# An attention and FFN block on one core: the row maxima transposed by VectorE instead of TensorE

## The reference

```python
qkv = jnp.einsum('bsd,ed->bse', x, W_qkv)
q, k = _rope(q, positions), _rope(k, positions)
scores = jnp.einsum('bhqd,bhkd->bhqk', q, k) / jnp.sqrt(jnp.float32(dk))
scores = jnp.where(causal, scores, -jnp.inf)
out = jnp.einsum('bhqk,bhkd->bhqd', jax.nn.softmax(scores, axis=-1), v)
x = _layernorm(x + out @ W_o.T)
x = _layernorm(x + x @ simulate_quantize_int4(kernel) + bias + (x @ a) @ b)
```

## Time and profile before

| | us |
|---|---|
| median of 3 runs | 448.7 (448.59 to 451.78) |
| the profiled execution | 448.93 |
| its span | 446.9 |
| busy: TensorE, VectorE, ScalarE, POOL | 419.6, 378.9, 317.4, 119.4 |

### The profile page before, as it was taken

How to read it: one execution, slowest core, us unless ns; L and a number is a source line. 1 busy time by engine, 2 the same in 40 slices (tenths; PEclk the granted TensorE clock), 3 DMA queues, 4 the chain that set the end, 5 groups by cost and what they waited for, 6 DMA issues and landing times.

```text
span 446.9 us, 8486 instructions
## 1 busy us (share of the span) xinstructions
PE 419.6 (94%) x3198; PEld 204.5 (46%) x3198; DVE 378.9 (85%) x491; ACT 317.4 (71%) x643; POOL 119.4 (27%) x188
## 2 busy tenths in 40 slices
PE   5989899799799999999999999999999999999873
PEld 2546445334334445454443544544353445535352
DVE  2888799899989999998999999899988898645476
ACT  2454884476477788767877888778898887999741
POOL 8879602102110210131121322012002011241655
PEclk9999999699899999999999999999999999999998
DMA  7522202121000012200000022200000000000001
GB/s 217 195 96 89 105 3 80 56 65 36 2 2 0 3 43 81 68 11 3 3 2 1 2 65 67 67 3 0 2 1 2 1 3 2 2 26 1 2 24 48
DMA packets 12200, 16.56 MB, mean 37 GB/s; under 512 B 2444, under 2 KB 7324, under 8 KB 12160
## 3 DMA queue, kind: packets, MB, share of 16 engines
q1 hardware_dynamic: 11072, 15.75, 11.1%
q0 software_dynamic: 1088, 0.28, 0.4%
HBM read 10.37 MB, written 5.24 MB: 35 GB/s over the span
## 4 chain that ended last, share of the span: by engine, by line
PE 76%; DVE 12%; ACT 5%; issue 3%; POOL 3%; DMA 1%; POOLq 0%; SPq 0%; DVEq 0%; ACTq 0%
PE ps L1289 26%; PE ps L1275 22%; PE ps L1231 16%; DVE pmax L1052 10%; ACT probs L974 4%; PE ps L1199 3%; PE ps L1298 2%; PE ps L1245 1%; POOL rstd L856 1%; PE ps L1205 1%; DMA x_sb<-in_L_attn_x_dram 1%; PE ps L1241 1%; PE ps L1215 1%; PE ps L1255 1%; DVE cs L1140 1%
## 5 line engine op out<-in xcount | busy, mean ns | idle before, releaser
L1052 DVE TENSOR_REDUCE pmax<-ps 128x2 f32<-128x1024 f32 (+3 forms) x273 | 318.9, 1216 | 36.6 <-PE ps L1231 19.1
L974 ACT ACTIVATE probs<-ps 128x512 f32<-128x512 f32 (+2 forms) x576 | 285.3, 583 | 81.7 <-PE ps L1275 79.5
L1275 PE MATMUL ps<-qS,kS 64*128 64x512 f32 (+3 forms) x648 | 167.0, 411 | 2.5 <-DVE pmax L1052 1.3
L1231 PE MATMUL ps<-kS,qS 64*128 64x512 f32 (+3 forms) x640 | 140.9, 416 | 7.2 <-DVE pmax L1052 3.7
L1289 PE MATMUL ps<-probs,vP 128*9 128x512 f32 (+3 forms) x1296 | 145.0, 530 | 1.2 <-POOL probs L881 1.1
L1275 PEld LDWEIGHTS ps<-qS,kS 64*128 64x128 f32 x648 | 84.1, 186 | 91.9 <-ACT probs L974 71.9
L1231 PEld LDWEIGHTS ps<-kS,qS 64*128 64x128 f32 x640 | 66.6, 186 | 58.7 <-DVE pmax L1052 26.1
L881 POOL TENSOR_SCALAR_AFFINE_SELECT probs<-probs 128x512 f32<-128x512 f32 x64 | 40.3, 636 | 150.5 <-ACT probs L974 150.2
L890 POOL DMA_DIRECT2D qS<-mrows x34 | 19.7, 581 | 138.4 <-DVE mrows L1072 138.3
L1289 PEld LDWEIGHTS ps<-probs,vP 128*9 128x9 f32 x1296 | 21.3, 89 | 42.1 <-issue 21.0
L1245 PEld LDWEIGHTS ps<-causal_x,ident_x 64*128 64x128 f32 x188 | 18.3, 186 | 0.0
(11 more groups left out here) (116 smaller groups left out, 197.4 us busy)
## 6 DMA issues: line engine op xcount, KB each, us to landing
qS<-q_parts SPq DMA_DIRECT2D x52, 64.0 KB
kS<-k_parts SPq DMA_DIRECT2D x52, 64.0 KB
cs<-rope_tables_dram SPq DMA_DIRECT2D x4, 512.0 KB, 7.1
q_parts<-qp SPq DMA_DIRECT2D x4, 512.0 KB, 3.0
k_parts<-kp SPq DMA_DIRECT2D x4, 512.0 KB, 2.8
x_sb<-in_L_attn_x_dram SPq DMA_DIRECT2D x4, 256.0 KB, 6.8
out_dram<-rot SPq DMA_DIRECT2D x2, 256.0 KB, 2.3
qS<-mrows POOLq DMA_DIRECT2D x30, 8.0 KB, 1.8
```

Of the source, the lines that this page charges most:

```text
L974: nc.scalar.activation(probs[:, J % PRING, heads[0]:heads[-1] + 1:2, lo:hi], bank_of(("S", n, j, i))[:, 0:len(heads) * (hi - lo)].rearrang ...
L1052: nc.vector.tensor_reduce(dst, src, AX.X, ALU.max).then_inc(unit_free, 1)
L1231: last = nc.tensor.matmul(ps[:, HELD[e][hl], at:at + w], qS[rows, b, c, hp, ii * TOK:(ii + 1) * TOK], kS[rows, b, kk, hp, 0:w], start=i == ...
L1275: last = nc.tensor.matmul(bank_of(("S", n, j, i))[:, x * w:(x + 1) * w], kS[rows, b, j // TPC, hp, (j % TPC) * TOK:(j % TPC + 1) * TOK], q ...
```

## The change

VectorE turns the maxima itself. Its transpose works on squares of 32 by 32. It copies the 16 columns of `nmax` rounded into `mparts` and writes the remainder beside them: 32 columns, with the columns in the order in which the DMA wants the rows. Four transposes then put the four groups of 32 partitions side by side in `mrows`, 32 rows of 128 queries (16 rows in each of the two short tasks). One DMA of POOL carries all rows of a task (two in the last two tasks). TensorE has no M any more and no bank is held for it.

M stays in `SCHEDULE` as a step of VectorE and POOL, and the planner always puts it directly behind the task's last A. Its counts become 0.22 + 0.7 us of VectorE, none of TensorE, and `LANDING` 2.9. With these numbers it finds another order of the whole program.

```diff
-    return 2 if e[0] == "A" else int(e[0] in ("S", "M", "L", "O", "POST") or (e[0] == "PV" and e[2] == 0))
+    return 2 if e[0] == "A" else int(e[0] in ("S", "L", "O", "POST") or (e[0] == "PV" and e[2] == 0))
...
-    LANDING = 4.0
+    LANDING = 2.9
...
             if unit == units(n)[-1]:
-                self.dve += 0.22
-                self.due += ((self.dve + self.TO_PE, "M", n),)
+                self.dve += 0.22 + 0.7
+                self.side = (self.side[0], self.side[1] + 0.7)
+                self.ready = self.ready[:n] + (self.dve + self.LANDING,) + self.ready[n + 1:]
+                rows = n
...
-        elif kind == "M":
-            self.aside(0.25, 0.6, ready)
-            self.ready = self.ready[:e[0]] + (self.dve + self.LANDING,) + self.ready[e[0] + 1:]
...
+        if kind == "A" and rows is not None:
+            self.order = (self.order, max(begin, ready), self.dve, ("M", rows), ())
...
-        mrows = sb("mrows", [2 * PAIRS * TPC, 2, PARTS, CH // 2], fp32r)
+
+        mparts = sb("mparts", [128, 2, 32], fp32r)
+        mrows = sb("mrows", [32, 2, TOK])
...
-                for a in range(PARTS):
-                    pool.wait_ge(rows_done, PARTS * n + a + 1)
-                    at, (count, w) = SHIFT_AT + a * SHIFT_STEP, rows_of(n)
-                    pool.dma_start(qS[at:at + 2 * SHIFT_STEP + 1:2 * SHIFT_STEP, b, c, :, lo:hi].bitcast(fp32),
-                                 mrows[0:count, n % 2, a, 0:w].bitcast(fp32)).then_inc(mrow_in[b, c, first], 16)
+                pool.wait_ge(rows_done, 4 * (n + 1))
+                to, pieces = qS[SHIFT_AT:SHIFT_AT + 3 * SHIFT_STEP + 1:SHIFT_STEP, b, c, :, lo:hi].bitcast(fp32), row_pieces(n)
+                for i in range(pieces):
+                    count = 2 * PARTS * PAIRS * (end - first) // pieces
+                    pool.dma_start(to if pieces == 1 else to[:, i, :], mrows[i * count:(i + 1) * count, n % 2, :]).then_inc(mrow_in[b, c, first], 16)
...
+            nc.vector.memset(mparts[:, :, :].bitcast(fp32), 0.0).then_inc(parts_set, 1)
...
             def rows(n):
-                e, (count, w) = ("M", n), rows_of(n)
-                src, to = bank_of(e)[0:count, 0:w], mrows[0:count, n % 2, :, 0:w]
-                dve.wait_ge(unit_done, UNIT[e])
+                tiles = TASKS[n][3] - TASKS[n][2]
+                whole, of = nmax[:, n % 2, 0:2 * PAIRS * tiles], mparts[:, n % 2, 0:2 * PARTS * PAIRS * tiles]
+                if row_pieces(n) == 1:
+                    whole, of = whole.rearrange("p (l r) -> p l r", l=2), of.rearrange("p (l a r) -> p a l r", l=2, a=PARTS)
+                else:
+                    whole, of = whole.rearrange("p (l h t) -> p l h t", l=2, h=PAIRS), of.rearrange("p (h l a t) -> p a l h t", h=PAIRS, l=2, a=PARTS)
+                dve.wait_ge(parts_set, 1)
+                dve.wait_ge(nmax_done, n + 1)
+                if n >= 2:
+                    dve.wait_ge(rows_done, 4 * (n - 1))
+                nc.vector.tensor_copy(of[:, 0], whole).then_inc(split_done, 1)
+                dve.wait_ge(split_done, PARTS * n + 1)
+                nc.vector.tensor_tensor(of[:, 1], whole, of[:, 0].bitcast(fp32), ALU.subtract).then_inc(split_done, 1)
+                dve.wait_ge(split_done, PARTS * n + 2)
                 if n >= 2:
                     rows_in(dve, n - 2)
-                nc.vector.tensor_copy(to[:, 0, :], src).then_inc(rows_done, 1)
-                dve.wait_ge(rows_done, PARTS * n + 1)
-                nc.vector.tensor_tensor(to[:, 1, :], src, to[:, 0, :].bitcast(fp32), ALU.subtract).then_inc(rows_done, 1)
+                for b in range(4):
+                    nc.vector.transpose(mrows[:, n % 2, 32 * b:32 * (b + 1)], mparts[32 * b:32 * (b + 1), n % 2, :].bitcast(fp32)).then_inc(rows_done, 1)
...
-            def maxima_rows(n):
-                e = ("M", n)
-                banks_taken(pe, e)
-                pe.wait_ge(nmax_done, n + 1)
-                count, w = rows_of(n)
-                for t in range(w // TOK):
-                    last = nc.tensor.transpose(bank_of(e)[0:count, t * TOK:(t + 1) * TOK], nmax[:, n % 2, t * count:(t + 1) * count], ident[:, :])
-                last.then_inc(unit_done, 1)
```

More of the change, by code:

```diff
@@ L313, in take @@
             self.a += 1
+            rows = None
             parts, masked = products(n, unit)
@@ L482 @@
 SCHEDULE = schedule()
-RING_EVENTS = ("A", "M", "L", "O", "POST")
+RING_EVENTS = ("A", "L", "O", "POST")
 UNIT = {e: i + 1 for i, e in enumerate(e for e in SCHEDULE if e[0] in RING_EVENTS)}
@@ L609, in attention_block @@
         rows_done = sem("rows_done")
+        split_done = sem("split_done")
+        parts_set = sem("parts_set")
         turned_copied = sem("turned_copied")
@@ L668, in attention_block @@
             elif e[0] in RING_EVENTS:
-                RELEASE[e] = (rows_done, PARTS * (e[1] + 1)) if e[0] == "M" else (unit_free, 1 + sum(s is unit_free for s, _ in RELEASE.values()))
+                RELEASE[e] = (unit_free, 1 + sum(s is unit_free for s, _ in RELEASE.values()))
             elif e[0] == "S":
@@ L691, in sets_done, with row_pieces @@
             return SET[(n, j, len(score_sets(n, j)) - 1)] + 1
-        def rows_of(n):
-            return (2 * PAIRS * TPC, TOK) if TASKS[n][3] - TASKS[n][2] == TPC else (2 * PAIRS, CH // 2)
+        def row_pieces(n):
+            return 1 if TASKS[n][3] - TASKS[n][2] == TPC else PAIRS
         def rows_in(eng, n):
             key = [(g % 2, c, first) for g, c, first, _ in TASKS]
-            eng.wait_ge(mrow_in[key[n]], 16 * PARTS * (1 + key[:n].count(key[n])))
+            eng.wait_ge(mrow_in[key[n]], 16 * sum(row_pieces(m) for m in range(n + 1) if key[m] == key[n]))
         LOADS, CLEARS = 16 * LOAD_PIECES, 16
@@ L1055, in row_max @@
                     if n >= 2:
-                        dve.wait_ge(unit_done, UNIT[("M", n - 2)])
+                        dve.wait_ge(split_done, PARTS * (n - 1))
                     of = pmax[:, :, :, area:area + (end - first) * SLOTS]
@@ L1062, in row_max @@
                     else:
-                        nc.vector.tensor_reduce(to.rearrange("p (t h) -> p h t", t=2), of.rearrange("p l h (t k) -> p (l h) t k", t=2),
+                        nc.vector.tensor_reduce(to.rearrange("p (h t) -> p h t", t=2), of.rearrange("p l h (t k) -> p (l h) t k", t=2),
                                                 AX.X, ALU.max, negate=True).then_inc(nmax_done, 1)
             def rows(n):
-                e, (count, w) = ("M", n), rows_of(n)
-                src, to = bank_of(e)[0:count, 0:w], mrows[0:count, n % 2, :, 0:w]
-                dve.wait_ge(unit_done, UNIT[e])
+                tiles = TASKS[n][3] - TASKS[n][2]
[12 more added lines that the diff above has]
+                dve.wait_ge(split_done, PARTS * n + 2)
                 if n >= 2:
                     rows_in(dve, n - 2)
-                nc.vector.tensor_copy(to[:, 0, :], src).then_inc(rows_done, 1)
-                dve.wait_ge(rows_done, PARTS * n + 1)
-                nc.vector.tensor_tensor(to[:, 1, :], src, to[:, 0, :].bitcast(fp32), ALU.subtract).then_inc(rows_done, 1)
+                for b in range(4):
+                    nc.vector.transpose(mrows[:, n % 2, 32 * b:32 * (b + 1)], mparts[32 * b:32 * (b + 1), n % 2, :].bitcast(fp32)).then_inc(rows_done, 1)
             def quantise():
@@ L1336, in _ @@
                     scores(*e[1:])
-                if e[0] == "M":
-                    maxima_rows(e[1])
                 if e[0] == "L":
```

## The result

The changed kernel takes 461.2 us (median of 4 runs, 460.5 to 464.1) where the one before takes 448.6 beside it: ratio **1.026** [1.021, 1.031] (fast runs alone, 95% interval), some 12 us slower. The forecast was 447.0 with a range up to 453. The profiled execution took 460.86, span 459.1.

The account below looks back on a forecast made before the run. VectorE was taken to set the pace up to about 150 us, TensorE after it. The terms -2.6 + 2.0 + 1.5 - 1.5 - 1.2 = -1.8 us, from 448.93, gave 447.0 us, range 442.5 to 453.

Parts of the forecast that it names:

- Queues: POOL's and SP's queues: the moved row DMA can hold a mask some 1 us, but products need it later: 0.
- the four rivals: Hand-overs carry in full 443.3 (0.20), VectorE bound 455.6 (0.13), scores too early 453.4 (0.10), no effect 449 us (0.07).
- TensorE, -2.6: TensorE loses its transposes of the maxima: 0.20 us in each of 13 tasks from task 4 on, -2.6 us.
- VectorE, +0.65 a task: VectorE's added time for cast, subtraction and four transposes: between +0.36 and +0.68 us a task, taken as +0.65.
- What of it counts, +3.5: VectorE's added time reaching the end: all at tasks 2 to 4 (+2.0 us), a quarter at tasks 5 to 13 (+1.5).
- The test that the prediction set itself: Forecast is wrong if VectorE's share of the path in 150:320 passes about 15%.
- the second rival: VectorE becomes the bound up to 380 us, added time of tasks 2 to 13 reaching the end: 455.6 us, chance 0.13.
- The hand-over, -1.5 and -1.2: Maxima to scores at tasks 2 and 3 shrinks to 3.3 us: -1.5 us, and -1.2 from less half clock behind it.
- the clock's gain of 1.2 us: TensorE's 10.2 us at half clock behind tasks 2 and 3, worth 5.1 us, counted at a quarter: -1.2 us.
- The third rival: Scores ordered too early, so TensorE waits for rows at tasks 1, 2 and 3: 453.4 us, chance 0.10.

Follow-up runs that it names:

- experiment 4: The changed kernel in its own order, but SP instead of POOL issues the row DMA: 451.3 us, ratio 1.001.
- experiment 12: The kernel before the change, its two row DMAs a task issued by SP instead of POOL: 447.3 us, ratio 0.995.
- experiment 9: The changed kernel with rows sent by SP, while POOL still waits for the transposes at the old place and sends nothing: 456.2 us, ratio 1.011.
- experiment 2: The changed kernel with four more transposes a task on VectorE into a tile nobody reads: 472.7 us, ratio 1.048.
- experiment 10: The changed kernel with rows sent by SP in four DMAs a task (eight in the short tasks), four transposes kept: 455.7 us, ratio 1.014.
- experiment 5: The changed kernel with rows sent by SP and four more unused transposes a task on VectorE: 469.0 us, ratio 1.040.
- experiment 8: The changed kernel with rows sent by SP, one transpose over 128 partitions instead of four, and four collecting DMAs: 449.4 us, ratio 0.998.
- experiment 11: As experiment 8, with the planner's LANDING 3.9 instead of 2.9: 445.6 us, ratio 0.990.

## Why the prediction was wrong

The 12 us come apart by experiments 4 and 12: 9 us (2.0%, ± 3 us) are what it costs the changed kernel more than the one before that POOL sends the rows, and 2.8 us are everything else together. Of the 9 us, POOL's waiting by itself is about half (4.4 us in experiment 9); the rest comes with the sending.

**The step that failed is "Queues".** The prediction saw that POOL would wait for the transposes ahead of task 3's masks, said "that can hold a mask some 1 us; the products that need it stand several units later: 0". At task 4 the mask began 2.7 us later than it could (by experiment 4's timing: with the score unit, 153.35; it did at 156.05), and the product stood right behind. The place was the one that the prediction named; the price was set at nothing without a row that shows how far behind the mask its product stood. It looked at one mask, too: at task 15 a norm stands behind the rows and holds VectorE, then TensorE. Put at 0, the term came to 3.5 us behind task 4, 1.0 behind task 11 and 5.1 behind task 15 (table of experiment 4), the low clock behind tasks 4 and 15 with it; in experiment 4 the clock is at 1.00 in both places. None of the four rivals had this mechanism. The one that ends nearest, 455.6, is VectorE's; its time is below the measured one.

**TensorE, -2.6:** the transposes are gone as said; their worth by themselves wasn't measured, so no run shows this term.

**VectorE, +0.65 a task:** +0.91. A transpose takes 0.20 us, the start to start is 0.23 and not 0.19, as each begins only after the last one's end: the rule of the Trainium skill that the prediction quoted ("VectorE: DVE Perf Modes", "Two Vector instructions with no wait between them") agrees with the trace, since the squares lie in different groups of 32 partitions and follow each other by their full length. The gaps ahead of the cast (75.39 to 75.48) and of the first square took 0.09 and 0.03 us.

**What of it counts, +3.5:** too small a share, the second step that failed. Experiments 2 and 10 put a microsecond of VectorE at 0.65 and 0.62, experiment 5 at 1.15, where the forecast had a third. It read that third from VectorE's share of the path before and from its idle time, 1.5 us in 30; and that VectorE is the path up to 150 us was read from 50:80 alone (in 80:110 it has 21% of the path before, in 110:150 31%). The test that the prediction set itself is a share of the path over 15%. The chain in 150:320, by line, of the kernel before and of the kernel with the rows by SP:

```profile
by line: PE ps L1289 34.5%; PE ps L1275 26.2%; PE ps L1231 19.0%; DVE pmax L1052 6.8%; ACT probs L974 6.4%; PE ps L1298 2.4%; PE ps L1245 1.5%; issue 1.4%; PE ps L1255 1.0%; PE ps L1241 0.6%; PE ps L1263 0.2%; ACTq L973 0.0%
...
by line: PE ps L1297 28.6%; PE ps L1283 24.4%; PE ps L1248 18.4%; DVE pmax L1059 12.8%; issue 3.1%; ACT probs L980 2.6%; DVE mrows L1091 2.4%; PE ps L1306 1.8%; PE ps L1258 1.4%; PE ps L1262 1.3%; DVE nmax L1067 1.0%; DVE mparts L1084 0.8%;
```

VectorE's four lines make 17.0%, after 6.8% before. In the change itself the share is not over 15%: VectorE has 11.5% there, the reductions 8.7 of them, and "issue", the chain through POOL, 18.0%. So the second rival, VectorE as a bound, was real in part, and the queue hid it. By 0.62 to 1.15 the 15.5 us would cost 10 us and more, but beside the kernel before only 2.8 are seen. The rest must be given back elsewhere; TensorE's lost transposes, the shorter hand-overs and the new order can do it, but no run separates them.

**The hand-over, -1.5 and -1.2:** 3.57 and 3.61 us where 3.3 was forecast. At task 2 the rows were ready 1.40 us behind the maxima and not 1.2, POOL's wake of 0.3 us was missed, and from issue to scores it took 1.87 us and not 2.1. The hand-over shrank by 1.85 and 0.67 us, but TensorE came to it with fewer units in hand and stood longer, and the low clock behind tasks 2 and 3 went from 6.8 + 3.4 to 6.8 + 6.8 us. So the clock's gain of 1.2 us didn't come, and the time was longer, not shorter, there. The reduction to the maxima of task 4 starts at 153.27, in the kernel before at 150.23; what of the 1.5 us arrived is not separated. The third rival had this right in kind: the wait for the rows themselves is 0.50 us at task 2, at task 3 it is 3.36 us.

## What to carry to other kernels

When a wait is moved within an in-order queue, list everything queued behind it and how far ahead of its consumer each stands; here a DMA that waits for another engine cost 2.5% more in the queue of the engine that also makes masks than in that of one that only sends, and the waiting alone 1.0%. Take the share of an engine's added time that arrives at the end from a run that doubles it, not from its share of the path before; and as three such comparisons here gave 0.62, 0.65 and 1.15, take it as rough. And where an instruction works on each group of 32 partitions by itself, give it all partitions at once and let the DMA sort the result, with the later landing told to whatever plans the order: without that it gained 0.3%, not clear of noise, with it 1.2% (experiments 8 and 11 against 4).
